# Differential attention with an expert-choice layer: all heads of batch 0 and then of batch 1, with batch 0's later stages laid into batch 1's

## The reference

```python
Q = proj(Wq); K = proj(Wk); V = proj(Wv)          # 8 heads of 2 x 128
A1 = einsum('bhqd,bhkd->bhqk', Q1, K1) * scaling
A2 = einsum('bhqd,bhkd->bhqk', Q2, K2) * scaling
attn = softmax(A1) - lam * softmax(A2)
O = einsum('bhqk,bhkd->bhqd', attn, V)
O = O / rms(O) * rms_scale * (1 - LAMBDA_INIT)    # rms over 256
x = layernorm(x + einsum('bne,de->bnd', O, Wo))
probs = softmax(x @ gate_w)                       # 8 experts
top_p, top_idx = top_k(probs of an expert over the tokens of a batch, 256)
h = gelu(xin @ w1[e]); y = (h @ w2[e]) * top_p    # xin: the chosen rows, hidden 512
x = layernorm(x + scatter_add(y))
```

## Time and profile before

| | |
|---|---|
| median of three runs | 1014.97 us |
| the profiled execution | 1011.95 us, its span 1010.1 us |
| TensorE busy | 864.1 us, 86% of the span |
| VectorE, ScalarE, GpSimd busy | 701.9, 726.1, 661.4 us |
| chain that ended last | TensorE 74%, GpSimd 8%, VectorE 7%, issue 5% |

### The profile page before, as it was taken

One profiled execution on the slowest core, in us unless ns is written; L12 is line 12 of the kernel. 1 busy time (PEld: TensorE's weight loads), 2 busy tenths in 40 slices (PEclk: granted clock), 3 DMA queues, 4 the chain that ended last, 5 costly groups with the idle time before them and its releaser, 6 DMA issues.

```text
span 1010.1 us, 15337 instructions
## 1 busy us (share of the span) xinstructions
PE 864.1 (86%) x4365; PEld 718.3 (71%) x4366; DVE 701.9 (69%) x1054; ACT 726.1 (72%) x1346; POOL 661.4 (65%) x1039
## 2 busy tenths in 40 slices
PE   5899999999999999999999999999998742288600
PEld 4678888888888888888888888888886531166400
DVE  5777777778777877787777777777775447666404
ACT  3889888988898888889888988898887332144100
POOL 3666767766676767776677667776776453278871
PEclk9999999999999999999999999999999955589755
DMA  2000000000000000000000000100000152012334
GB/s 73 1 22 1 1 1 22 1 0 0 21 0 0 21 0 0 0 21 0 0 0 21 0 0 0 52 0 1 1 1 1 54 136 68 14 50 41 32 37 125
DMA packets 36001, 20.67 MB, mean 20 GB/s; under 512 B 4560, under 2 KB 34416, under 8 KB 35968
## 3 DMA queue, kind: packets, MB, share of 16 engines
q1 hardware_dynamic: 30336, 15.95, 5.6%
q0 software_dynamic: 5632, 4.33, 3.1%
HBM read 13.85 MB, written 6.42 MB: 20 GB/s over the span
## 4 chain that ended last, share of the span: by engine, by line
PE 74%; POOL 8%; DVE 7%; issue 5%; ACT 2%; DMA 2%; POOLq 0%; SPq 0%; DVEq 0%; ACTq 0%
PE t_ps L1065 11%; PE ring_a L1013 6%; PE ring_a L1015 6%; PE ring_a L1014 6%; PE u_ps L1013 6%; PE u_ps L1015 6%; PE ring_b L1013 6%; PE ring_b L1015 6%; PE u_ps L1014 6%; PE ring_b L1014 6%; POOL acc_dram L514 4%; POOL prob L506 2%; PE o_ps L1014 2%; PE o_ps L1015 2%; PE o_ps L1013 2%
## 5 line engine op out<-in xcount | busy, mean ns | idle before, releaser
L473 POOL TENSOR_TENSOR attn<-prob 128x1024 f32<-128x1024 f32 x128 | 307.2, 2400 | 186.3 <-ACT prob L614 148.6
L793 DVE TENSOR_TENSOR at_lo<-t_ps,at_hi 128x512 fp32r<-128x512 f32 x256 | 176.1, 688 | 128.3 <-ACT at_hi L566 127.8
L784 DVE TENSOR_REDUCE negmax<-ring_a 128x1 f32<-128x1024 f32 x128 | 156.8, 1225 | 58.4 <-PE ring_a L1015 55.5
L566 ACT ACTIVATE at_hi<-t_ps 128x512 fp32r<-128x512 f32 x256 | 153.7, 600 | 52.8 <-PE t_ps L1065 51.2
L1065 PE MATMUL t_ps<-ident,attn 128*128 128x128 f32 x1024 | 154.0, 272 | 6.8 <-DVE at_lo L793 6.4
L784 DVE TENSOR_REDUCE negmax<-ring_b 128x1 f32<-128x1024 f32 x128 | 156.2, 1220 | 1.6 <-PE ring_b L1015 0.6
L1065 PEld LDWEIGHTS t_ps<-ident,attn 128*128 128x128 f32 x1024 | 126.6, 141 | 32.7 <-DVE at_lo L793 6.6
L579 ACT ACTIVATE prob<-ring_a,negmax 128x1024 f32<-128x1024 f32 x128 | 143.3, 1120 | 7.4 <-DVE negmax L784 5.4
L614 ACT ACTIVATE prob<-prob,coef 128x1024 f32<-128x1024 f32 x128 | 147.9, 1156 | 0.0
L579 ACT ACTIVATE prob<-ring_b,negmax 128x1024 f32<-128x1024 f32 x128 | 142.6, 1114 | 0.3 <-DVE negmax L784 0.3
L1013 PE MATMUL ring_b<-xt_hi,q_hi 128*128 128x512 f32 x256 | 111.6, 436 | 0.9 <-ACT prob L579 0.9
(11 more groups left out here) (252 smaller groups left out, 1674.1 us busy)
## 6 DMA issues: line engine op xcount, KB each, us to landing
attn<-in_L_ffn_w SPq DMA_DIRECT2D x16, 256.0 KB, 3.1
xres<-in_L_attn_X SPq DMA_DIRECT2D x2, 512.0 KB, 4.4
wq_s<-in_L_attn_Wq SPq DMA_DIRECT2D x8, 128.0 KB, 2.3
wk_s<-in_L_attn_Wk SPq DMA_DIRECT2D x8, 128.0 KB, 2.4
wv_s<-in_L_attn_Wv SPq DMA_DIRECT2D x8, 128.0 KB, 2.0
wo_s<-in_L_attn_Wo SPq DMA_DIRECT2D x8, 128.0 KB, 2.4
acc_dram<-zero SPq DMA_DIRECT2D x1, 1024.0 KB, 5.1
xg_dram<-xres SPq DMA_DIRECT2D x2, 512.0 KB, 4.3
```

What stands on the lines that cost most here:

```text
L473: pool.tensor_tensor(attn[:, r % AB, :], prob[:, sp, 1, :], prob[:, sp, 0, :], ALU.add).then_inc(attn_ready, 1)
L566: act.activation(at_hi[:, g, half * GT:(half + 1) * GT, c], t_ps[:, 0:NC].rearrange("p (k q) -> p k q", q=P), ACT.Copy).then_inc(at_hi_don ...
L784: dve.tensor_reduce(negmax[:, par, m:m + 1], ring[m][:, :], axis=AX.X, op=ALU.max, negate=True).then_inc(negmax_ready, 1)
L793: dve.tensor_tensor(at_lo[:, g, k, c], t_ps[:, 0:NC].rearrange("p (k q) -> p k q", q=P), at_hi[:, g, k, c].bitcast(F32), ALU.subtract).the ...
```

## The change

The order of the work is new, and every engine's program is written out in full, with no loop left.

- There are 16 steps, the eight heads of batch 0 and then those of batch 1, each of eight slots (G = 0 to 127). M and W' of a head are made twice, once for each batch. X, Wv and Wo come also in a transposed layout, so TensorE's transposes of X and of the weights go. W' and Wv are written straight to one of two `ww` buffers, which ends ScalarE's two copies a head.
- Batch 0's layer norm lies in slots 77 to 82, the gate in 85 to 90, its rows' transposes in 93 and 94, the search (eight levels, the first of four probes and the others of sixteen, where there were ten of eight) in 95 to 103, ties and indices in 103 to 111, and its 16 gathers in 112 to 127.
- The end of attention is its own sequence, with outputs in eight different banks.
- The experts run as 16 jobs of 256 rows, batch 0's and then batch 1's, each in two halves; `ffn(n)` is one half on each engine: the downward product of half n-2, the upward one of half n, two Gelu passes on ScalarE (one to `g_hi`, rounded, where VectorE had cast it before), and the low part on VectorE. Batch 1's gate lies between ffn(0) and ffn(3), and each of the eight levels of its search holds one half: 4 to 11. Its ties and indices lie between ffn(12) and ffn(15).

The core of the diff (a removed line has `-`, an added one `+`):

```diff
@@ the schedule @@
...
-    X_QB = {0: (0, 0), 1: (1, 0), 2: (0, 1), 4: (1, 1)}
-    X_M, X_WT, X_WP, AT_WW = 5, 6, 8, 13
-    X_QA = {9: (0, 0), 10: (1, 0), 12: (0, 1), 13: (1, 1)}
-    AT_LN = (21, 22, 23, 24, 25)
+    X_M = 0
+    X_Q = {1: (0, 0), 2: (1, 0), 3: (0, 1), 4: (1, 1)}
+    X_WP = 7
+    AT_WT = 6
+    G_SUM = BT + LAG_O
+    G_CENT, G_SQ, G_SSQ, G_FAC, G_END = G_SUM + 1, G_SUM + 2, G_SUM + 3, G_SUM + 4, G_SUM + 5
+    G_XT = (85, 86)
+    G_GATE = 88
+    G_EXP, G_REP = 89, 90
+    G_ROWS = (93, 94)
+    G_LEV = 96
+    G_LIM, G_OFF, G_TOK = G_LEV + LEVELS, G_LEV + LEVELS + 1, G_LEV + LEVELS + 2
+    G_CUM = (109, 110)
+    G_GATHER = 112
@@ order of the heads @@
...
-        def heads(eng, slot):
-            for i in range(TPH):
-                slot(0, i, True, False, False)
-            with eng.Fori(1, H - 1) as h:
-                for i in range(TPH):
-                    slot(h, i, False, False, False)
-            for i in range(TPH):
-                slot(H - 1, i, False, True, False)
-            for i in range(TPH, TPH + LAG_Y):
-                slot(H - 1, i, False, True, True)
+        def exists(t):
+            return 0 <= t < TILES
@@ SP @@
...
+            for k in range(1, STEPS):
+                if k + 1 < STEPS:
+                    load_qk(k + 1)
+                if k == 11:
+                    store_x1(0)
+                if k == 12:
+                    store_pn(0)
+                    store_rows(0)
+                    load_vals(0)
+                load_vo(k)
@@ GpSimd @@
+            for G in range(TILES):
+                if exists(G - LAG_C):
+                    factor(G - LAG_C)
+                if exists(G - LAG_O):
+                    norm(G - LAG_O)
+                if exists(G - LAG_C):
+                    combine(G - LAG_C)
+                if G == G_FAC:
+                    ln_factors(0)
+                if G >= G_GATHER:
+                    n = G - G_GATHER
+                    if n == 0:
+                        gather_ready(0)
+                    gather_rows(n // CT, n % CT)
+            norm(115)
+            factor(127)
+            combine(127)
+            for t in range(116, 120):
+                norm(t)
             w_lower(0)
-            for n in range(1, B):
-                ln_factors(n)
-            for e in range(1, E):
-                w_lower(e)
...
-            pool.wait_ge(xg_stored, 16 * B)
-            pool.wait_ge(pn_stored, 16 * B)
-            pool.wait_ge(acc_stored, 16 * (B + 1))
-            for e in range(XSLOTS):
-                gather(e)
+            w_lower(1)
+            for t in range(120, TILES):
+                norm(t)
+            ln_factors(1)
+            w_lower(2)
+            w_lower(3)
+            w_lower(4)
             scatter(0)
-            for e in range(XSLOTS, E):
-                gather(e)
-            for e in range(1, E):
-                scatter(e)
-            for n in range(B, 2 * B):
-                ln_factors(n)
+            w_lower(5)
+            scatter(1)
+            w_lower(6)
+            scatter(2)
+            w_lower(7)
+            scatter(3)
+            scatter(4)
+            gather_ready(1)
+            for q in range(E, E + 4):
+                for k in range(CT):
+                    gather_rows(q, k)
+            for q in range(E + 4, JOBS):
+                if q - E + 1 < E:
+                    scatter(q - E + 1)
+                for k in range(CT):
+                    gather_rows(q, k)
+            for q in range(E, JOBS):
+                scatter(q)
+                if q == E + 5:
+                    ln_factors(2)
+            ln_factors(3)
@@ ScalarE, the end @@
+            at_high(124, 0)
+            exponential(127, 1)
+            u_high(29)
+            out_square(115)
+            at_high(124, 1)
+            at_high(125, 0)
+            at_high(125, 1)
+            at_high(126, 0)
+            scale(127)
+            at_high(126, 1)
+            u_high(30)
+            at_high(127, 0)
+            out_square(116)
+            out_square(117)
+            at_high(127, 1)
+            out_square(118)
+            out_square(119)
             w_round(0)
+            w_round(1)
+            u_high(31)
+            for t in range(120, TILES):
+                out_square(t)
+            xs_round(0)
+            act.activation(tick[:, 0:1], eps_c[:, :], ACT.Gelu).then_inc(ticked, 1)
             ln_squares(1)
+            ffn(0)
+            ffn(1)
+            x1t_copy(1, 0)
+            x1t_copy(1, 1)
+            ffn(2)
+            act.activation(tick[:, 1:2], eps_c[:, :], ACT.Exp).then_inc(ticked, 1)
+            gate_exps(1)
+            ffn(3)
@@ VectorE, a slot @@
+            for G in range(TILES):
+                k, s = (G - 1) // QT, (G - 1) % QT
+                if exists(G - LAG_T1 - 1):
+                    at_low(G - LAG_T1 - 1, 0)
+                row_max(G, 0)
+                if s in X_Q and k + 1 < STEPS and G > 0:
+                    q_part(k + 1, *X_Q[s], x_ps[:, :])
+                if s == X_M and k + 1 < STEPS:
+                    m_parts(k + 1, x_ps[:, 0:2 * D])
+                if s == X_WP and k >= 0:
+                    wp_parts(k)
+                if G == 1:
+                    for n in range(NCH, 2 * NCH):
+                        xt_lower(n)
...
+                if G == G_GATE or G_LEV <= G <= G_TOK:
+
+                    dve.wait_ge(fac_ready, G - LAG_O + 1)
+                if G == G_GATE:
+                    gate_max(0)
+                if G_LEV <= G < G_LEV + LEVELS:
+                    level_step(0, G - G_LEV)
+                if G == G_LIM:
+                    ties_limit(0)
+                if G == G_OFF:
+                    ties_offset(0)
+                if G == G_TOK:
+                    token_copy(0)
+                if exists(G - LAG_O):
+                    add_out(G - LAG_O)
+                if G == G_SUM:
+                    ln_total(0)
+                if G == G_CENT:
+                    ln_center(0)
+                if G == G_SSQ:
+                    ln_sums(0)
+                if G == G_END:
+                    ln_end(0)
+                if G == G_EXP:
+                    gate_norm(0)
+                if G == G_REP:
+                    gate_rep(0)
+                if G_LEV - 1 <= G < G_LEV + LEVELS - 1:
+                    level_count(0, G - G_LEV + 1)
+                    level_base(0, G - G_LEV + 1)
+                if G == G_LEV + LEVELS - 1:
+                    ties_count(0)
+                if G == G_LIM:
+                    ties_choose(0)
+                if G == G_OFF:
+                    ties_pick(0)
+                if G == G_TOK:
+                    ties_spread(0)
+                if G - 1 in G_CUM:
+                    indices(0, G_CUM.index(G - 1))
@@ VectorE, the end @@
+            ln_total(1)
+            ln_center(1)
             xs_lower(0)
+            ln_sums(1)
+            ln_end(1)
+            ffn(0)
+            ffn(1)
+            gate_max(1)
+            ffn(2)
+            gate_norm(1)
+            gate_rep(1)
+            ffn(3)
+            dve.wait_ge(rows_ready, 3)
+            dve.tensor_copy(rows[1][:, 0:NC], t_ps[:, :]).then_inc(rows_copied, 1)
+            for lv in range(LEVELS):
+                level_count(1, lv)
+                level_base(1, lv)
+                ffn(4 + lv)
+                level_step(1, lv)
+            ties_count(1)
+            ffn(12)
+            ties_limit(1)
+            ties_choose(1)
+            ties_offset(1)
+            ties_pick(1)
+            ties_spread(1)
+            ffn(13)
+            token_copy(1)
+            ffn(14)
+            indices(1, 0)
+            indices(1, 1)
+            for n in range(15, 28):
+                ffn(n)
+            add_parts(2)
+            ln_total(2)
+            ffn(28)
+            ln_center(2)
+            ffn(29)
+            ffn(30)
+            ln_sums(2)
+            for n in range(31, 34):
+                ffn(n)
+            ln_end(2)
+            ffn(34)
+            add_parts(3)
+            ln_total(3)
+            ln_center(3)
+            ln_sums(3)
+            ln_end(3)
@@ TensorE, a slot @@
+            for G in range(TILES):
+                k, s = G // QT, G % QT
+                scores(G, 0, 0)
+                scores(G, 0, 1)
+                if G == G_GATE or G_LEV <= G <= G_TOK:
+                    pe.wait_ge(y_added, G - LAG_O)
+                if G == G_GATE:
+                    gate(0)
+                if G_LEV <= G < G_LEV + LEVELS:
+                    votes(0, G - G_LEV)
+                if G == G_LIM:
+                    limit(0)
+                if G == G_OFF:
+                    offset(0)
+                if G == G_TOK:
+                    tokens(0)
+                t = G - LAG_O
+                if exists(t):
+                    need(pe, y_added, t)
+                    output(t)
+                if exists(G - LAG_T2):
```

(43 more changed lines are left out.)

1703 lines of the change are left out of this document (881 added, 822 removed).

## The result

The changed kernel is slower: 1046.4 us median (1045.16 to 1048.3, 4 runs) against 1016.36 (1010.0 to 1024.04) beside it, ratio 1.029 with a 95% interval of 1.022 to 1.037. The forecast was 1038 us, in a range of 992 to 1064, with 0.64 for slower. The profiled execution's span is 1043.4 us, 33.3 longer than before.

What follows compares the result with a forecast made beforehand. TensorE was taken to bound attention, and chains, longest GpSimd's queue, the 238 us behind it. Attention's terms summed to +33 us and the tail got only 7 shorter, giving 1038 us, range 992 to 1064.

Steps and rivals of the forecast that it cites:

- Start: Start of attention: fewer transposes and an earlier lambda, but two casts before the first row maximum; -2 us (-5 to +2).
- M and W' twice: Attention: M and W' made 16 times instead of 8, less four transposes a head; +2.5 us (0 to 5).
- Levels and ties of batch 0: Slots 95 to 105: search work exceeds VectorE's idle time, so TensorE's next scores come late; +17 us (6 to 27).
- rival 1: Slower still: in 11 attention slots two-input VectorE instructions wait for GpSimd's sum, 26 us, total 1064; chance 0.14.
- Norm, gate, indices: Attention: batch 0's layer norm, gate, transposes and indices do not fit wholly; +8 us (4 to 14).
- Gathers: Last 16 attention slots: a gather behind each GpSimd sum makes its chain 6.1 us; +7.5 us (0 to 21).
- End of attention: From last exponential to last addition: ScalarE sets the order; 26.5 us (21.5 to 32), where it was 36.
- From the last addition to the first count: Batch 1's layer norm, gate and rows, between ffn(0) and ffn(3), before its search; 24.5 us (20 to 29).
- Search: Batch 1's search: each level holds its steps and an expert half in series, 8.5 us; 68 us (55 to 78).
- Ties: Batch 1's ties and indices: ffn(12), (13) and (14) in series between their steps; 24 us (18 to 28).
- Queue and end: From batch 1's first gather: GpSimd's 16 gathers and 22 scatters, then loads, norm and store; 88 us (82 to 95).
- what would show it: Expected trace signs: sum spacing in attention, batch 1's counts 7 to 10 us apart near half clock, gapless GpSimd queue.

Runs made afterwards that it cites:

- e2_u_first: Changed kernel with u rounded on ScalarE before q, and u's low part first on VectorE: 1036.3 us, ratio 1.021 to the kernel before.
- e7_one_input: Changed kernel with the search's 128x1 ORs as tensor_scalar, one input from SBUF: 1030.9 us, ratio 1.012 to the kernel before.
- e5_all: Changed kernel with step before half, u first, gather before sum, batch 0's levels spread, batch 1's ties and indices earlier: 992.2 us, ratio 0.974 to kernel before.
- e1_step_first: Changed kernel with batch 1's search step ahead of VectorE's part of the expert half: 1017.3 us, ratio 1.002 to the kernel before.

## Why the prediction was right, and where it was not

Direction and range are right, and most terms with them; the forecast was 8 us too low. It was not as close as that sounds: attention was forecast 11 us too short and the tail 4 too long, which cancels in part, and the range is 72 us wide. By its own steps, with the length between the same two sums in the kernel before taken off:

- **Start**: -4.7 us at the first sum (28.43 to 23.72), forecast -2, bound -5.
- **M and W' twice**: forecast +2.5 (0 to 5; 16 x 0.45 less 8 x 0.55 is 2.8), in fact +8.9 up to sum 72 alone, at 1.16 a step; carried on over the 54 slots left it is +16.7, of which 7.8 are an estimate. This is the term that was mis-sized and the only one outside its bounds. The products cost what was said, about 4 (e2_u_first); the rest is the wait for `u`, since the doubled parts now fall in the slots in which `u` is rounded, and stand ahead of it in the code of two engines. I had costed the products on TensorE and not asked what their casts on ScalarE and VectorE are put in front of.
- **Levels and ties of batch 0**: +17 forecast, +18.5 measured (sums 94 to 106, 0.145 a slot taken off for the weights). That the sum fits is luck in part, for its reason is not the one found. 11 of it were ORs that stood still (e7_one_input), which is rival 1's mechanism. The other 7.4, which my reason could still claim, lie where four instructions of the ties are held for 7.5 us, and no run tells the two apart. Rival 1 priced the held time at 2.4 us in each of eleven slots, 26 us. Over all of attention it was 26.2, in seventeen instructions, of which 11 are shown to lie on the path. Rival 1 put its 26 on top of a sum that had already laid the whole overrun of these slots to VectorE's load, so its 1064 was too late. Both could be partly true at once, which the list of cases had not allowed.
- **Norm, gate, indices** of batch 0: +8 forecast, +10.3 (sums 72 to 94 and 106 to 112). The pass over 1024 numbers that was to "fit almost" took 3.13 us instead of 1.23. **Gathers**: +7.5 forecast, +3.9 (sums 112 to 126); slots of 6.13 to 6.19 in most of them where 6.1 was forecast, but the slots before averaged 5.79 there, not 5.55.
- Together +44.7 (-4.7 + 8.9 + 7.8 + 18.5 + 10.3 + 3.9) instead of +33; the last exponential came 44.1 later.
- **End of attention** 27.1 (26.5 forecast). From the last addition to the first count 21.9 (24.5 forecast). **Search**: 57.0 from the first to the eighth count, a pitch of 8.1 us, forecast 8.5, and for the reason given: the step stands behind the half, at a granted clock of 0.56. The parts that the prediction lists add up to 7.1 us at half clock, and to 7.7 to 8.0 with the mean of what comes in every other level; they do not give its 8.8, and 8.1 is nearer to them. **Ties**: from the last OR of the search, 929.4, to the first gather 23.1, forecast 24. **Queue and end** 90.9 (70.1 + 20.8), forecast 88. So the tail is 226.9 where 231 was forecast.
- Of what would show it, two signs failed: the sums up to slot 76 were to be 5.5 to 6.3 us apart, and in each eight two were 6.70 and 6.48; slots 96 to 105 were to be 7 and averaged 7.7, between 6.8 and 8.7.

GpSimd's queue was expected to be 39 us shorter and is 37 (106.8 to 70.1), since 16 gathers lie in attention and 10 scatters go ahead of it. That was spent on a search of 57.0 us from first to last count, which had taken 26.5 for both batches together (835.03 to 861.54), and on a longer attention.

## What to carry to other kernels

When work is laid into another chain, look at each in-order engine for what now stands between a result and its use: here one line's place was worth 27 us, while the overlap had made the whole tail only 11 shorter. A small instruction beside a long one of GpSimd is not small if both of its inputs are in SBUF; give it a per-partition scalar, and look whether it is then short in the trace, or expect the length of the other. Price all such instructions that a change puts beside GpSimd's, and not only those of one loop: here seventeen were held. Removing one held instruction may only uncover the next, or a wait that it had covered, so price the engine's queue, not the instruction. A schedule that loses may be three local faults away from one that wins: 1.029 became 0.983 with the three, and 0.961 with the rest.

## What the runs showed of the hardware

- A 128x1 OR of two SBUF tiles took 0.15 to 3.79 us (the longest in e5_all), as a `tensor_scalar` with a scalar per partition 0.20 to 0.22 always. In the row with 3.68 VectorE's record even begins 0.57 us ahead of GpSimd's (880.26 and 880.83) and both end together; GpSimd's spans are rough.
- One input is not always enough. In the change this `tensor_scalar` of 8 columns, which takes 0.17 in batch 1's norm (844.86), ends at 482.18, with GpSimd's sum (479.75, 2.40 long). Whether it ran in a mode with two ports no row shows.

```profile
480.92 1.26 DVE L907 TENSOR_SCALAR stat<-stat 128x8 f32<-128x8 f32 x1
```

- GpSimd is held too: behind the sum that held the norm's pass of 3.13 us, its next instruction, 128x1, took 1.54 us where it mostly takes 0.54 to 0.56.
- A matmul of 256 columns, not in the trace before, is issued each 0.12 us at full clock and each 0.21 at half (granted clock 1.00 from 870.4 to 870.9, 0.50 from 876.2 to 877.2), half of the 0.23 and 0.43 for 512 columns. In the changed kernel:

```profile
870.45 0.28 PE L1255 MATMUL ring_a<-xk_lo,q_hi 128*128 128x256 f32 x1
870.57 0.28 PE L1256 MATMUL ring_a<-xk_hi,q_lo 128*128 128x256 f32 x1
...
876.77 0.41 PE L1256 MATMUL ring_b<-at_hi,q_lo 128*128 128x256 f32 x1
876.98 0.41 PE L1254 MATMUL ring_b<-at_hi,q_hi 128*128 128x256 f32 x1
```

- In the search TensorE's granted clock was 0.59 with 7.53 us of work in 20; where the same halves came closer together (e1_step_first, 860 to 880: 12.62 of 20) it was 0.83.
